# A clear on GpSimd behind each block's gathers, sixteen gathered tiles, and scatters eight steps behind the gathers

## The reference, cut to what matters

```python
x = _layernorm(x + _L0_gnn_ref(...))   # two graph convolutions, 128 wide
x = _layernorm(x + _L1_gnn_ref(...))   # gated messages from x[dst], x[src] and the edge's attributes
x = _layernorm(x + _L2_gnn_ref(...))   # attention with three heads
x = _layernorm(x + _L3_gnn_ref(...))   # six graph convolutions, 64, 32, 16, 32, 64, 128 wide, then h @ Wf + bf

def _gcn_conv(h, W, b, row, col, norm, num_nodes):
    h = h @ W
    msg = h[row] * norm[:, None]
    agg = jax.ops.segment_sum(msg, col, num_segments=num_nodes)
    return agg + b
```

## Time and profile before

| | before |
|---|---|
| median of three runs | 11513.55 us (11469.03 to 11515.87) |
| profiled execution | 11609.91 us, its span 11608.2 us |
| busy: DVE, POOL, PE, ACT | 69%, 64%, 57%, 51% |
| mean rate of the DMA engines | 146 GB/s over the span |
| gathers and scatters issued by GpSimd | 5497 indirect DMAs |
| chain that ended last | its list names some 11% of the span, 5% of it "another core or an unknown queue" |

### The profile page before, as it was taken

The page is one execution under the profiler, slowest core; times in us unless marked ns, Lnnn a source line. Parts: engine busy times, 40 slices in busy tenths (PEclk is TensorE's granted clock), DMA queues, the critical chain, the costliest instruction groups (busy, mean ns, idle before and its releaser), DMA issues. The chain is left out here.

```text
span 11608.2 us, 141508 instructions
## 1 busy us (share of the span) xinstructions
PE 6579.4 (57%) x32436; PEld 5426.1 (47%) x32436; DVE 8028.9 (69%) x33105; ACT 5915.6 (51%) x13869; POOL 7392.5 (64%) x6801
## 2 busy tenths in 40 slices
PE   6036666656664666677656665754455565643343
PEld 3035556645554666677646665642233343422222
DVE  7347799956667999899888884445466666764444
ACT  0024467757667999898667772321133232322222
POOL 7734478867776888666467764556545555556666
PEclk8568888878886555688778885555577555655555
DMA  4977678832224777444345553433344333322221
GB/s 137 302 241 237 235 268 290 289 114 71 71 70 139 236 234 236 144 141 140 107 139 176 176 172 107 136 102 83 85 128 132 89 98 88 120 85 55 56 58 54
DMA packets 1019495, 1694.44 MB, mean 146 GB/s; under 512 B 304877, under 2 KB 535080, under 8 KB 1018594
## 3 DMA queue, kind: packets, MB, share of 16 engines
q1 hardware_dynamic: 782752, 1361.06, 35.0%
q0 software_dynamic: 175936, 218.82, 8.4%
q10 hardware_dynamic: 59970, 105.49, 2.7%
HBM read 988.03 MB, written 707.78 MB: 146 GB/s over the span
## 5 line engine op out<-in xcount | busy, mean ns | idle before, releaser
L1340 POOL DMA_INDIRECT g_got<-scaled,row_src x2352 | 2230.9, 949 | 1651.4 <-issue 679.7
L298 PE MATMUL g_a_p_z<-sb_L_gnn_W,g_a_u_t 128*128 128x128 f32 (+3 forms) x2574 | 653.1, 398 | 1046.4 <-ACT g_a_u_t L1185 375.4
L902 DVE SCALAR_TENSOR_TENSOR g_sums<-g_got,first,g_sums 128x128 f32<-128x128 f32 (+3 forms) x3136 | 869.1, 277 | 395.0 <-issue 111.4
L298 PEld LDWEIGHTS g_a_p_z<-sb_L_gnn_W,g_a_u_t 128*128 128x128 f32 (+1 forms) x2574 | 483.6, 266 | 1219.5 <-issue 562.4
L906 DVE SCALAR_TENSOR_TENSOR g_sums<-g_sums,cont,g_got 128x128 f32<-128x128 f32 (+3 forms) x3128 | 884.7, 283 | 121.6 <-DVE g_sums L902 91.9
L1185 ACT COPY g_a_u_t<-g_a_p_t 128x512 f32<-128x512 f32 (+3 forms) x495 | 225.3, 455 | 1350.4 <-remote 735.5
L298 PE MATMUL g_bb_p_z<-sb_L_gnn_W,g_bb_u_t 128*128 128x128 f32 (+2 forms) x4302 | 836.2, 362 | 121.8 <-DVE g_bb_z L1077 78.6
L298 PEld LDWEIGHTS g_bb_p_z<-sb_L_gnn_W,g_bb_u_t 128*128 128x128 f32 x4302 | 755.8, 262 | 170.9 <-issue 141.7
L1185 ACT COPY g_bb_u_t<-g_bb_p_t 128x1024 f32<-128x1024 f32 (+2 forms) x294 | 233.8, 795 | 1143.2 <-PE g_bb_p_t L289 591.1
L1340 POOL DMA_INDIRECT g_got<-xs,idx_src x392 | 370.8, 946 | 481.4 <-DVE g_a_own L1021 271.3
L1252 POOL DMA_INDIRECT out<-g_a_o,idx_out x396 | 395.3, 998 | 351.6 <-ACT g_a_o L350 222.3
(11 more groups left out here) (495 smaller groups left out, 23743.0 us busy)
## 6 DMA issues: line engine op xcount, KB each, us to landing
raw<-gb_u SPq DMA_DIRECT2D x98, 768.0 KB
xs<-f_o ACTq DMA_DIRECT2D x97, 516.0 KB
f_x<-in_x ACTq DMA_DIRECT2D x97, 512.0 KB
g_bb_own<-in_x SPq DMA_DIRECT2D x97, 512.0 KB
wide<-g_bb_o SPq DMA_DIRECT2D x97, 512.0 KB
g_bb_own<-wide SPq DMA_DIRECT2D x97, 512.0 KB
g_bb_res<-in_x SPq DMA_DIRECT2D x97, 512.0 KB
x<-g_bb_o SPq DMA_DIRECT2D x97, 512.0 KB
```

The costliest lines, as they stand in the source:

```text
L298: last = nc.tensor.matmul(dst_psum[0:p, q * g * width:(q * g + n) * width], turned_tile[0:n * k, q * P:q * P + p], weight[0:n * k, 0:n * w ...
L902: nc.vector.scalar_tensor_tensor(out=self.firsts, in0=new, scalar=first[:, col], in1=self.firsts, op0=ALU.mult, op1=ALU.add).then_inc(run_ ...
L1340: pool.indirect_dma_start(got[b.s4][:, c * row:(c + 1) * row], None, table, bass.IndirectOffsetOnAxis(ap=index[:, b.n * CH + c:b.n * CH + ...
```

## The change

Three constants are added: `RING` = 16, `OUT_RING` = 8, `REST` = 1024.

- In every `graph_pass` the gathered tiles become sixteen. A gather waits for the sum of block b - 16 and for the landing of the gathers of block b - 4, in place of the sum of block b - 4.
- A stage `rest` clears a tile `idle` of 128 x 1024 f32 on GpSimd; nothing reads it. It stands behind each block's gathers in g1, g3 to g7 and `gated_edge_pass`, and in g8 behind each block's gathers and behind each block's scatters. Each clear waits for the end of the one before. g2 gets none.
- In g8 the scatters run eight steps behind the gathers, with eight output tiles; a scatter waits for the scatters of four blocks before, and `normalise` for those of eight blocks before.

```diff
+RING = 16
+OUT_RING = 8
+REST = 1024
-                dve, tile = nc.vector, self.tiles[b.s4 % len(self.tiles)]
+                dve, tile = nc.vector, self.tiles[b.n % len(self.tiles)]
-                self.o_s = [sb(f"{n}_o{s}", [P, G * m]) for s in range(UNROLL if scatters else 2)]
+                self.o_s = [sb(f"{n}_o{s}", [P, G * m]) for s in range(OUT_RING if scatters else 2)]
-                    if b.after(UNROLL):
-                        nc.scalar.wait_ge(scattered[b.s4], past(scattered[b.s4]) + b.turn * CH * DMA)
+                    if b.after(OUT_RING):
+                        nc.scalar.wait_ge(scattered[b.s4], past(scattered[b.s4]) + (b.turn + 1 - OUT_RING // UNROLL) * CH * DMA)
                 nc.gpsimd.wait_ge(self.m_.finished, b.n + 1)
+                if b.after(UNROLL):
+                    nc.gpsimd.wait_ge(scattered[b.s4], past(scattered[b.s4]) + b.turn * CH * DMA)
-                        self.o_s[b.s4][:, c * D:(c + 1) * D], None, bounds_check=N - 1, oob_is_err=False
+                        self.o_s[b.n % OUT_RING][:, c * D:(c + 1) * D], None, bounds_check=N - 1, oob_is_err=False
-                got = [sb(f"got{s}", [P, CH * row]) for s in range(UNROLL)]
+                got = [sb(f"got{s}", [P, CH * row]) for s in range(RING)]
+                idle = sb("idle", [P, REST])
+                        rests = Steps(pool_step, 999)
+                        def rest(b):
+                            if rests.k:
+                                pool.wait_ge(pool_step, rests.k)
+                            nc.gpsimd.memset(idle[:, :], 0.0).then_inc(pool_step, 1)
+                            rests.count()
                         def gather(b):
                             if b.after(UNROLL):
-                                pool.wait_ge(mark_a.combined, b.n - UNROLL + 1)
+                                pool.wait_ge(gathered[b.s4], past(gathered[b.s4]) + b.turn * CH * DMA)
+                            if b.after(RING):
+                                pool.wait_ge(mark_a.combined, b.n - RING + 1)
                                 if keep_rows:
-                                    pool.wait_ge(indexed, b.n - UNROLL + 1)
+                                    pool.wait_ge(indexed, b.n - RING + 1)
...
-                                    got[b.s4][:, c * row:(c + 1) * row], None, table,
+                                    got[b.n % RING][:, c * row:(c + 1) * row], None, table,
...
                         if scatters:
-                            pipeline(pool, [(gather, 0, NBE), (na.scatter, 4, NBA)])
+                            pipeline(pool, [(gather, 0, NBE), (rest, 0, NBE), (na.scatter, 8, NBA), (rest, 8, NBA)])
...
                         else:
-                            pipeline(pool, [(gather, 0, NBE)])
+                            pipeline(pool, [(gather, 0, NBE), (rest, 0, NBE)])
...
+                idle = sb("idle", [P, REST])
...
+                                if rests.k:
+                                    pool.wait_ge(pool_step, rests.k)
+                                nc.gpsimd.memset(idle[:, :], 0.0).then_inc(pool_step, 1)
+                                rests.count()
```

More of the change, by code:

```diff
@@ L1376, in keep_row @@
                             dve.wait_ge(gathered[b.s4], gathers_before(gathered[b.s4], b))
-                            nc.vector.tensor_copy(at_window(row_src, b), got[b.s4][:, k:CH * row:row]
+                            nc.vector.tensor_copy(at_window(row_src, b), got[b.n % RING][:, k:CH * row:row]
                                                   ).then_inc(indexed, 1)
```

## The result

The changed kernel takes 11207.8 us (median of four, 11195.4 to 11240.6) against 11508.5 (four, 11469.0 to 11515.9) on the same chip: ratio 0.9749, 95% interval 0.9730 to 0.9768. The forecast was 11050 us, 4.0% less, with a range of 10900 to 11400. Its profiled execution has a span of 11193.4 us.

The account below looks back on a forecast made before the run. Held semaphore updates, not full engines, were taken to bound the touched passes; with pauses, GpSimd's list would. Seven graph passes and the gated pass's -30 made -467 us, taken from the median 11513.55: 11050 us, range 10900 to 11400.

Parts of the forecast that it names:

- The mechanism: While GpSimd issues long bursts of indirect DMAs, other engines' semaphore updates are held, coming through about 1 us after the burst.
- The second rival: Only an idle GpSimd lets updates through; if a clear isn't a pause, six passes slow, +590 us, 12100; chance 0.07.
- The third rival: Late starts have another cause, such as a DMA queue; clears only lengthen GpSimd's list, about 11580 us; chance 0.06.
- the gated pass: Pass with eight gathers a block: 11.5 us a block with one clear against 11.6; -30 us taken, bounds +78 and -80.
- GpSimd's list: GpSimd's own work in the graph passes, expected to become the bound once most "remote" time goes.
- the floor: Least time for a block of four gathers with its clear on GpSimd: 5.8 us.
- The sum of the seven graph passes: g1 -103, g3 -87, g4 0, g5 -101, g6 -35, g7 -34, g8 -77 us.
- the bound I had named: Gated pass, worst case: all clears added, +78 us.
- the sixteen tiles: Remove GpSimd's wait for the sum of block b - 4, at no cost; nothing counted in g2, 16 us at most.
- The first rival: Pause too short: the burst's backlog outlasts 1.10 us and updates go on being held; about 11360 us; chance 0.17.
- One of its signs: For the pause too short: gathers wait for the sum of b - 16; also "remote" waits of 5 to 12 us.
- the surplus: The profiled execution's 11610 us lies 96 us above the runs' median 11513.55; the -467 was taken from the median.

## Why the prediction was right, and where it wasn't

**The mechanism.** It was right: updates come late while GpSimd issues, and the clears let them through. Two runs show it best: the clears alone, with four tiles, give 0.9664, and the changed kernel with clears half as long is slower than with long ones (1.0099 against 0.9749) with less work on GpSimd. The prediction's sign for "right", no or small "remote" rows in g3 to g8, came true in g4 and g8 alone; elsewhere such waits of up to 8.3 us went on.

The second rival falls by g4 and g8 of the changed kernel: GpSimd waits for nobody there and the late time is 0, so a clear is a pause. The third rival, a cause that the clears don't touch, falls: g8's late time went from 877 us to 0 with clears, and the gated pass's from 247 to 0. The load of the DMA engines isn't it either: before, their share was 0.21 in g8 and 0.80 in g2, whose late time is 1 us. What no run separates is GpSimd's issuing from the transfers that it starts, since a pause spaces out both.

By the Trainium skill, page "SBUF — State Buffer", section "Who interferes with whom", "PE and ACT never wait on anyone". That is about ports. For semaphore updates these runs show the opposite: 497 of g8's 877 us are waits of ScalarE.

**GpSimd's list.** The clear was put at 0.94 us and measures 0.971; the pause 1.10, measured 1.13; the floor 5.8 a block, measured 5.81. g8 was put at -77 and moved by -71.

**The sum of the seven graph passes** was -437 and is -440 in the profiles. That it fits so well is luck, since its terms are not all right. g1, g3 and g5 gained 19, 26 and 14 us less, g4, g6 and g7 18, 25 and 25 more. I took the gathers' pace for the pass; g1's gathers ran at 6.17 a block, faster than the 6.6 I gave, and then GpSimd sat through 97.4 us until the others were done. The waits at the end of g1:

```profile
POOL g_got L1357 <- POOLq L180: 97.4, 1, 97.4
```

**The gated pass** is the step that failed: -30 forecast, +78 measured. I read the clear as standing behind a block's eight gathers. It stands inside the loop over the two tables, behind each four. The section on the change has the same mistake. My count of 785 clears left the gated pass out altogether; there are 981. The timeline of the pass:

```profile
2900.69 1.08 POOL L1513 DMA_INDIRECT cg_got_src<-x,row_src  x1 [0.30 <-issue]
2901.76 0.98 POOL L1519 MEMSET cg_idle<- 128x1024 f32 x1
2902.90 0.95 POOL L1513 DMA_INDIRECT cg_got_dst<-x,row_dst  x1 [0.16 <-issue]
```

With two clears the working of the prediction gives 10.7 + 1.6 = 12.3 a block, and 12.49 came, with no late update left and GpSimd as the only bound. That +78 is also the bound I had named is chance: it stood for one clear a block added in full. By the time to the next pass's first gather the clears cost 59 us against before, and taking them out gave 74 back.

**What the sixteen tiles do.** I had them at nothing, or a help. They cost: 0.9664 without them, 0.9749 with them, the clears being the same. A GpSimd that waits for sums has pauses longer than the clear's: over 1.3 us behind 67 of 97 bursts in g1 and 9 in g5 with clears only, 46 and 0 in the changed kernel. The tiles take them away, and a marginal pause is all that is left. The counts agree with this, no run tests it by itself. With 1280 columns the difference is gone but for g1.

**The first rival, the pause too short,** was half right. I gave it 0.17 and a price of all or nothing. In truth 1.13 us is at the edge: 0 us of late time in g4 and g8, 146 to 247 in g1, g3 and g5 of the changed kernel, and on another chip it misses more. One of its signs was there too: in g3 GpSimd waited nine times, 9.3 us in all, for a sum sixteen blocks back.

**From profile to median.** The two profiled executions differ by 414.8 us, the medians by 300.7. I took the working from the profiled execution, 96 us above the median of the runs, and subtracted it whole from the median. The 414.8 are 440 less in the graph passes, 59 more in the gated pass, 31 less in the first pass (682 and 651 us), which the change doesn't touch, and 3 less in the rest. As for the surplus, the profile of before looks like one from a slower chip: in the pass over attention scores TensorE's first late update comes 1.02 us after a burst of four, near the third chip's 1.04, where the profile of the changed kernel has 0.96. That is likely, not shown; its time is none of the four that the ratio rests on. The surplus and the gated pass are why 2.5% came and not 4.0%: -467 with the gated pass at +59 is -378, and 300.7 was measured.

## What to carry to other kernels

When engines start long after the instruction they waited for has ended, look at what GpSimd issues at that time. Indirect DMAs in long bursts can be worth breaking up with a pause of 1.1 to 1.35 us behind every four, even by work that nobody needs; measure the length on more than one chip, since 1.13 us, nearly enough on two chips, was too short on the third. Deeper buffers for such gathers were no help by themselves here: without pauses they made the kernel 2.4% slower.

## What the hardware showed

- Late updates go with GpSimd's issuing. Before, of the updates of TensorE and VectorE that ScalarE and VectorE waited for, 793 of 1469 came over 0.5 us late where their instruction ended while GpSimd issued indirect DMAs, and 28 of 703 where it ended 1.2 us or more behind GpSimd's last one. After, it is 381 of 1173 and 0 of 507, worked out from semaphore times.
- In the graph passes updates come later the longer the burst. In the kernel before, TensorE's first late update comes 1.1 us after the last indirect DMA's end with 4 of them (median, 80 bursts), 1.8 with 8 (41), 2.4 with 12 (48), 4.4 with 32 (11); some 0.12 to 0.16 us for each DMA more. In the gated pass, whose gathers take longer to issue, it grows less: 1.2 with 8 (32), 1.5 with 16 (29). Within a long burst some come through after 8 to 20 us.
- Late time doesn't follow the transfer's size: it is 269 us in g1, whose gathered rows are 129 wide, and 220 in g4, whose rows are 32 wide. It is greatest in g8, where gathers and scatters alternate. Neither size nor direction was varied by itself.
- TensorE's updates make up most of the late time, but VectorE's come late too: 149 us of g4's late time before are VectorE's waits for VectorE. What holds them inside the chip isn't shown by any run.
- The time differs from chip to chip: 0.94 to 0.96 us after a burst of four on two chips and 1.04 on a third, in a pass that no kernel changed.
- In the gated pass now and then an indirect DMA takes 1.2 to 2.0 us to issue, not 0.95, with pauses or without; the mean there is 1.04 before and 1.05 after.
